# A planner that lists one core's work takes its units by shifted numbers

## The reference, cut to what matters

```python
x = x + L0(x, cond)     # shared: silu(x@w1)*(x@w3)@w2; routed: sum of gate_e * gelu(x@W1e)@W2e
x = x + L1(x, cond)     # the same with two shared experts
# L2, for t = 0..255, h0 = cond:
gate = sigmoid(h @ Wh.T + z_t @ Wz.T + b)
h = tanh(h * leak + gate * z_t)          # the output of step t
x = x + hs
# L3, 16 heads of 8 features:
scores = q @ k.T / sqrt(8); softmax over keys that are not later; out = attn @ v
x = x + out @ c_proj_w + c_proj_b
```

## Time and profile before

| | us |
|---|---|
| time, median of 3 runs (439.58 to 440.62) | 439.76 |
| the profiled execution's own time | 439.82 |
| its span, first to last instruction | 437.8 |
| PE busy | 414.9 (95%) |
| DVE busy | 291.6 (67%) |
| ACT busy | 249.4 (57%) |
| POOL busy | 86.2 (20%) |
| first and last SCAN start | 43.7 and 339.2 |

### The profile page before, as it was taken

One profiled execution on the slowest core, in us unless ns is written; L12 is line 12 of the kernel. 1 busy time (PEld: TensorE's weight loads), 2 busy tenths in 40 slices (PEclk: granted clock), 3 DMA queues, 4 the chain that ended last, 5 costly groups with the idle time before them and its releaser, 6 DMA issues.

```text
span 437.8 us, 13080 instructions
## 1 busy us (share of the span) xinstructions
PE 414.9 (95%) x4568; PEld 306.4 (70%) x4568; DVE 291.6 (67%) x983; ACT 249.4 (57%) x869; POOL 86.2 (20%) x366
## 2 busy tenths in 40 slices
PE   2999999899999999999999999899999999999994
PEld 2777877767777778777566767657765776777772
DVE  5875665877566665666458766447753987996662
ACT  3642664554663664654755447575657555756881
POOL 6320321231231331222322123121111000000000
PEclk9999999999999999999999999999999999999998
DMA  8510000000000000000000000000000100100001
GB/s 299 199 20 9 5 1 1 1 2 1 1 2 1 1 2 2 1 1 1 2 1 0 2 3 3 0 2 4 2 2 3 26 3 6 24 4 4 10 23 25
DMA packets 11222, 7.70 MB, mean 18 GB/s; under 512 B 8983, under 2 KB 10263, under 8 KB 11159
## 3 DMA queue, kind: packets, MB, share of 16 engines
q1 hardware_dynamic: 10727, 6.61, 4.9%
q10 hardware_dynamic: 432, 0.27, 0.2%
HBM read 5.39 MB, written 1.05 MB: 15 GB/s over the span
## 4 chain that ended last, share of the span: by engine, by line
PE 80%; ACT 9%; DVE 7%; issue 2%; DMA 1%; POOL 1%; DVEq 0%; ACTq 0%
PE ybk L1068 18%; PE cbk L1242 12%; PE hid L1221 10%; PE ybk L1193 6%; PE vbk L1221 4%; DVE cbk L1568 3%; PE hid L1119 3%; PE cbk L1246 2%; PE hid L1094 2%; ACT hb L916 2%; PE hid L1169 2%; ACT dd L990 2%; PE hid L1053 2%; PE cbk L1169 2%; ACT hs L995 1%
## 5 line engine op out<-in xcount | busy, mean ns | idle before, releaser
L1568 DVE TENSOR_TENSOR_SCAN cbk<-dd 128x24 f32<-128x24 f32 x256 | 55.6, 217 | 100.3 <-ACT dd L990 96.8
L1242 PEld LDWEIGHTS cbk<-hs,rec 128*128 128x128 f32 x512 | 76.3, 188 | 55.8 <-ACT hs L995 47.3
L1068 PE MATMUL ybk<-hg,down 128*128 128x256 f32 x352 | 100.3, 400 | 0.8 <-DVE hg L1447 0.5
L806 POOL TENSOR_TENSOR dd<-hs,leak 128x8 f32<-128x8 f32 x256 | 55.7, 218 | 229.2 <-ACT hs L995 225.5
L1242 PE MATMUL cbk<-hs,rec 128*128 128x8 f32 x512 | 92.5, 253 | 4.7 <-ACT hs L995 1.8
L995 ACT ACTIVATE hs<-cbk 128x8 f32<-128x8 f32 x256 | 45.3, 177 | 65.6 <-DVE cbk L1568 64.4
L990 ACT ACTIVATE dd<-cbk 128x8 f32<-128x8 f32 x256 | 46.4, 181 | 55.6 <-PE cbk L1242 54.6
L1221 PE MATMUL hid<-xsp,up 128*128 128x256 f16 x486 | 70.9, 277 | 0.4 <-DVE lg L1386 0.3
L1068 PEld LDWEIGHTS ybk<-hg,down 128*128 128x128 f32 x352 | 58.7, 191 | 6.3 <-DVE hg L1447 1.6
L1221 PEld LDWEIGHTS hid<-xsp,up 128*128 128x128 f16 x486 | 46.7, 106 | 8.7 <-issue 0.7
L1447 DVE TENSOR_TENSOR hg<-hb,hid 128x512 f32<-128x512 f32 x50 | 33.5, 676 | 2.6 <-PE hid L1053 2.5
(11 more groups left out here) (235 smaller groups left out, 658.2 us busy)
## 6 DMA issues: line engine op xcount, KB each, us to landing
qz<-up_in SPq DMA_DIRECT2D x3, 512.0 KB, 7.4
out_dram<-silu SPq DMA_DIRECT2D x4, 256.0 KB, 3.1
x<-x_in SPq DMA_DIRECT2D x7, 128.0 KB, 9.4
down<-down_in SPq DMA_DIRECT2D x1, 768.0 KB, 9.6
att<-att_in SPq DMA_DIRECT2D x1, 743.0 KB, 10.7
down<-down_in SPq DMA_DIRECT2D x1, 640.0 KB, 6.1
kp<-mrow SPq DMA_DIRECT2D x32, 4.0 KB
qz<-rows SPq DMA_DIRECT2D x32, 2.0 KB, 1.7
```

The source lines that it names most:

```text
L806: tts(dd[:, t % ZR, 1, :, 2], hs[:, t, :], leak[:, 0:1].broadcast_to([P, B]), ALU.mult).then_inc(decay, 1)
L1068: m = pe.matmul(ybk[l][:, 0:n], D(l, "w2" if shared else "e2", e * f + i), hg[:, hg_of[made] % NHG, i * n:i * n + n], start=first and i == ...
L1242: pe.matmul(cbk[c % 2][:, o:o + B], wh, hs[:, t, :], start=False, stop=True, skip_group_check=True).then_inc(gate_pre, 1)
L1568: nc.vector.tensor_tensor_scan(vps[chunk_of(t) % 2], dd[:, t % ZR, 0].rearrange("p b o -> p (b o)"), dd[:, t % ZR, 1].rearrange("p b o -> ...
```

## The change

A table LATER is added, with one signed shift for each *block* of units, 246 of them. `block_of()` says which block a unit belongs to: most kinds by chunk and layer, or by quarter and pair of batches. A unit's number becomes its place plus its block's shift, and at least 0. Nothing else is changed: the units, what each needs, the costs, the order inside a queue and the steps' number -1 stay. The four lists come out in another order, and with them the PSUM banks, the buffer turns, the counts in the waits and the fillers. Shifts go from -589 to 791. The core of the diff (the lines left out hold more shifts of the same kind):

```diff
--- before.py
+++ after.py
@@ -69,6 +69,50 @@
 ENGINES = ("pe", "act", "dve", "pool")
 SLACK = {"pe": .1, "act": .05, "dve": .05, "pool": .1}
 WINDOW = {"pe": .88, "act": .45, "dve": .88, "pool": .88}
+LATER = {('A', 0, 0): -4, ('A', 0, 1): -40, ('A', 0, 2): 10, ('A', 0, 3): 8, ('A', 1, 0): -21, ('A', 1, 1): -3,
...
+         ('AV', 0, 0): -18, ('AV', 0, 1): -405, ('AV', 0, 2): 28, ('AV', 0, 3): -151, ('AV', 1, 0): 261,
...
+         ('C', 0): -271, ('C', 2): 22, ('C', 3): -216, ('C', 4): 20, ('C', 5): -365, ('C', 7): -16,
+         ('E', 0, 0): -519, ('E', 0, 1): -580, ('E', 1, 0): 1, ('E', 1, 1): 9, ('E', 2, 0): -14, ('E', 2, 1): 24,
...
+         ('E', 6, 1): 12, ('E', 7, 0): 19, ('E', 7, 1): -177, ('G', 0, 0): -159, ('G', 0, 1): -123, ('G', 1, 0): 8,
...
+         ('IK',): 34, ('K', 0): -54, ('K', 2): 44, ('K', 3): -200, ('M', 0, 0): -391, ('M', 0, 1): -299,
+         ('M', 1, 0): 8, ('M', 1, 1): 8, ('M', 2, 0): 11, ('M', 3, 1): -23, ('M', 4, 0): 2, ('M', 5, 0): 8,
...
+         ('O', 2): 174, ('O', 3): -16, ('Q', 0): -5, ('Q', 1): -30, ('Q', 2): 33, ('Q', 3): -161, ('QZ', 0): -58,
...
+         ('W',): 63, ('X', 0, 0): -126, ('X', 0, 2): 93, ('X', 0, 3): 29, ('X', 1, 0): 4, ('X', 1, 1): -74,
+         ('X', 2, 0): 1, ('X', 2, 1): 462, ('X', 2, 2): 4, ('X', 2, 3): 791, ('X', 3, 0): -216, ('X', 3, 1): -18,
...
+         ('Y', 2, 0, 'e'): -24, ('Y', 2, 0, 's'): -17, ('Y', 2, 1, 'e'): -21, ('Y', 2, 1, 's'): -15,
+         ('Y', 3, 0, 'e'): 389, ('Y', 3, 0, 's'): -22, ('Y', 3, 1, 'e'): 384, ('Y', 3, 1, 's'): 391,
...
+         ('YL', 3): -31, ('YL', 5): 97, ('YL', 6): -81, ('YL', 7): 78, ('Z', 0): 10, ('Z', 1): 76, ('Z', 2): -17,
+         ('Z', 3): -19, ('Z', 4): 60, ('Z', 5): 149, ('Z', 6): 2, ('Z', 7): -14}


 def columns(*parts):
@@ -174,12 +218,35 @@
     return {"XS": 15.0, "IK": 25.0, "MB": 12.0}.get(key[0], 7.0)


+
+def block_of(key):
+
+    k = key[0]
+    if k in ("R", "RT", "RS", "RD", "RC", "RG", "GT"):
+        return "G", key[1], key[2]
+    if k in ("SA", "SB"):
+        return "SH", key[1], key[2]
+    if k == "Y":
+        return key[:4]
+    if k in ("E", "M", "YE", "AC", "X"):
+        return key[:3]
+    if k in ("K", "KP", "Q", "QP", "V"):
+        return k[0], key[1]
+    if k == "X3":
+        return k, key[1] // QT
+    if k in ("MT", "L", "EI"):
+        return "MT", key[1], key[2]
+    if k in ("A", "S", "SC", "AV"):
+        return "S" if k == "SC" else k, key[1], key[2] // 2
+    return key[:1] if k in ("VI", "W") else key[:2]
+
+
 def schedule(units):

     chain = [(kind, t) for t in range(T) for kind in ("DECAY", "STEP", "GATE", "SCAN", "NEW")]
     needs, banked, number, queues = {}, set(), {}, {}
     for n, (key, bank, need) in enumerate(units):
-        needs[key], number[key] = need, n
+        needs[key], number[key] = need, max(0, n + LATER.get(block_of(key), 0))
         if bank:
             banked.add(key)
     for key in chain:
```

## The result

The changed kernel takes 424.23 us (median of 4 runs, 423.10 to 426.60), beside 440.16 us (439.58 to 440.62) for the kernel before. The ratio is 0.965 with an interval of 0.960 to 0.969: 15.9 us less, where 5.2 us less was forecast. The profiled execution is the slowest of the four (426.60 us, span 424.8 us), so its rows show 13.2 us of the gain; the other three took 2.3 to 3.5 us less.

A forecast was written before the change was run, and what follows sets the result against it. Bound by the front, the steps' latency and work left after the last step; -0.5 (front) - 5.2 (work beside steps) + 1.0 (step length) - 0.5 (tail) = -5.2 us from 439.82 gave 434.6 us, range 429.0 to 442.5 us.

The forecast's parts named there:

- late chunk: Recurrence: chunk 3's delayed Y makes its chunk 3 us too late and stops the steps; 442.8 us, chance 0.10.
- nothing: Whole kernel: the same units compete and leftover lumps go to the next slot; time stays at 439.8 us, chance 0.10.
- more switches: PE: finer mixing adds ten weight-load waits between tiled and full units, 0.3 us each; 442.8 us, chance 0.08.
- Front: Before the first step: chunk 0's units win ties, steps start sooner; -0.5 us, bounds 2 us gain and 1 us loss.
- Length of the steps: The 256 recurrence steps: fuller slots add under three more overfull ones; +1.0 us, bounds -1 and +4 us.
- Work beside the steps: Slots between steps, 220 to 339.5 us: better mixing saves half the fillers' 10.5 us of PE; -5.2 us.
- the tail's sum: After the last step: tail shorter than 93.5 us from 98.6; wrong if shrinking much less or more than fillers x 0.107 us.
- signs of being right: Second-part fillers 50 or fewer, last SCAN within 1.5 us of 339.2, tail under 93.5 us, first SCAN 42.5 to 43.7 us.
- Tail: After the last step: earlier K and Q of quarter 3 let ACT's exps start sooner; -0.5 us, bounds -3 and +2 us.
- More of the same: Steps and front: four fifths of the fillers' time (8.4 us) plus 1 us from the front; 430.4 us, chance 0.14.

The follow-up runs named there:

- the searched table: New table of 226 shifts, searched on the planner's estimate with corrected costs, fillers left out, against the kernel before: 420.97 us, ratio 0.958.
- the end fillers of the searched kernel: 14 fillers added in the waits of the last X, TR and O to the newly searched order with 54 fillers: 421.44 us, ratio 0.958 to the kernel before.
- the one with 54 fillers in its emptiest slots: Newly searched order with 54 fillers, only where work between two steps is below 0.4 us, against the kernel before: 420.80 us, ratio 0.957.

## Why the prediction was wrong, step by step

**Sign and mechanism were right.** The latency of the steps plus the work left over sets the time; an order moves work from the tail beside the steps. The runs carry that through: over all profiled executions, the tail is PE's busy time in it plus 5.7 to 7.8 us (98.6 and 92.2, 101.8 and 94.0, 96.3 and 90.3, 88.2 and 81.6, 85.4 and 77.9, 81.4 and 75.2). The late chunk, nothing and more switches did not happen.

**Front, forecast -0.5 us:** -1.0 us, inside its bounds, but executions of one order differ by up to 0.7 us there. The run with the experts' shifts alone had it at 41.9, 1.8 us sooner. The prediction misread one pair of entries: the shifts of chunk 1's first Y block are -6 and -78, not -61 and -78, so only its routed part gets 0, the shared one 62.

**Length of the steps, forecast +1.0 us:** +1.2 us, a match that owes something to luck. The forecast put three more overfull slots where attention work runs, behind 220 us; there the steps took 1.184 us each (119.6 / 101) after 1.183. The growth came before it: 177.3 / 155 = 1.144 us after 1.137. And other executions of the same order gave 296.9 and 297.8 us where this one gave 296.7. The run without fillers shows that the 69 that are left cost 2.4 us of the steps' length, and the prediction had given fillers no price. The table load still stands in the steps, at 250.15 instead of 274.13.

**Work beside the steps, forecast -5.2 us, is the step that failed.** With the tail's own -0.5 us it was to shorten the tail by 5.7 us; it shortened by 13.2, more than the bound of 10.5 us. Three things were mis-sized, in this order:

1. I took half of a bound. The fillers of the second stage fell from 98 to 49, which is exactly that half, 49 x 0.107 = 5.2 us. This part came out as written.
2. The bound left out the first stage. The prediction named its 5.5 us of fillers and gave them to a rival. They fell from 51 to 20: 3.3 us more. Work of the experts that is done sooner lets attention's run sooner, so that stage counts in the end too; that link is argued, with 64 matmuls of Y behind 220 us before and 60 now as its only sign. With it the sum is 8.6 us.
3. There was room in which no filler stood, and a filler may be worth more than 0.107 us. PE's busy time in the tail fell by 92.19 - 77.88 = 14.3 us, 5.7 us more than the 8.6; against the 75.15 us that the same 1632 matmuls took at 0.98 it fell by 17.0 us. Beside the steps, PE's idle time went from 295.50 - 288.12 = 7.38 us to 296.70 - 291.76 = 4.94 us, and the steps became 1.2 us longer: 2.4 + 1.2 = 3.6 us of room that no filler stood for, which makes 12.2 us. The rest lies in the size of a filler. As busy time the 149 fillers took 8.46 + 16.15 = 24.6 us, 0.165 us each, and the 69 took 11.5 us; 13.1 us less instead of 8.6 makes 16.7 us in all. A part of a filler's busy time overlaps the next matmul's, so 12.2 and 16.7 us are the two ends of this count, and where in between a filler's true size puts it stays open. No run varied the fillers' 0.62 us by itself. The 0.73 us of the earlier trace rows lie 0.11 us above it, 28 us over 256 slots, but with 7.4 us of idle time in the whole stage most of that wasn't free.

What was to show the tail's sum wrong, that it shrinks by much more than the fillers x 0.107 us, is what happened. All signs of being right came true as well: 49 fillers, the last SCAN 0.2 us from where it was, a tail under 93.5 us, the first SCAN at 42.7 us. They had no upper end, so they could not tell a gain of 5.2 us from one of 15.9. In the profiled execution the tail shrank by 1.1 us less than PE's work in it (13.2 against 14.3 us), as PE stood idle for 7.5 us of it instead of 6.4; what the clock of 0.94 costs is already in the 77.88 us.

**Tail, forecast -0.5 us:** the reason given, K and Q of quarter 3, was worth nothing. The overlap of the engines in the tail is no better than before, as these 6.4 and 7.5 us show.

**A late chunk:** the shift has its effect, C is 4.5 us later and 6 of 10.5 us of slack are gone, but no step waited. I had counted a loss of 12 steps; the argument against the rival, that the buffers run dry and leave Y alone, would explain why it was less, but no trace was read for it. I had not seen that the same shift could be needed for the gain.

**More switches:** PEld's waits for issue in the tail, all rows of that view added, were 9.2 us in 37 and are 10.6 us in 34. The prediction's "12 for 3.7 us" added only the two rows and was too low. Three of the largest rows after:

```profile
PEld ybk L1260 <- issue: 3.9, 10, 1.3
PEld cbk L1266 <- issue: 1.1, 2, 0.9
PEld cbk L1186 <- issue: 0.7, 4, 0.2
```

There are no more such gaps than before. Part of the 3.9 us is a single gap of 1.16 us before AV at 413.28. The Trainium skill, page TensorEngine Tiling (Array Packing), section Key Properties, says that a change of tiling mode drains TensorE; the gaps of 0.2 to 0.3 us agree, and no run here shows that the new order pays for more of them. The Trainium skill, page Perfetto Trace Analysis, section Optimization Strategy, says that interleaving regimes with different most contended engines may help. The trace agrees: beside the steps, where no engine but the latency sets the pace, DVE's busy time rose from 187.1 to 201.8 us with PE's matmuls, and in the tail it fell from 74.3 to 60.3.

**The chances.** "More of the same", four fifths of all fillers, had 0.14 and was the nearest case, and still 6 us short. I had the ends of all terms at 423.3 us and ruled them out because "fuller slots and longer steps go together". They did, but by 1 us against 14.

What stays open: which picks of the walk make the difference; no run tells. That the planner's estimate keeps the ranking nearly (405.8, 416.2, 418.1, 419.4, 422.6, 423.8, 424.8 against 424.2, 432.1, 437.3, 435.8, 440.8, 440.2, 445.0 us) says that a fit on it transfers to the chip, 16 to 20 us too low; but the searched table, 407.0 by corrected costs, brought no more than leaving the fillers out. Whether 420.8 us is near the floor of this tiling is not known.

## What to carry to other kernels

Where a greedy planner sets the order, don't price its entries one by one: the tail's PE busy time and the number of matmuls beside the latency-bound part say what an order is worth, and even a random perturbation of its tie-breaks can win 2%. Bound the gain by all the unused time of the scarce engine in the whole latency-bound part, the busy time of its fillers and its idle time (24.6 + 7.4 us here), not by a slot price for the fillers of one half of it. After such a change try the fillers again: with full slots they cost more than they brought here, with emptier ones they held the clock. And look at what the kernel beside it really did before a run is called a test: the end fillers of the searched kernel held a clock that had not fallen.

## What the runs showed of the hardware that was not expected

- 69 filler matmuls of 128x256 cost the steps 2.4 us (296.7 against 294.3 us), 0.035 us each, in one execution of each; without them the granted clock stayed at 1.00 beside the steps. In the old order, leaving out the 149 cost 5.3 us, with a granted clock of 0.65 to 0.87 in seven stretches of 10 us.
- The clock at the end of the kernel differs from one order and execution to another: the last pair of O took 2.05 us in the profiles of the changed kernel (granted clock 0.50 there), of the one with one shift set to 0 and of the searched one without fillers, 1.44 us without quarter 3's shifts and 1.10 us in the others without end fillers. Fillers that held it (1.12 us) made no difference that shows: 424.99 us with them, 424.23 us without.
- The spread of a kernel's runs followed its mean clock: 419.50 us at 0.992 and 423.84 us at 0.977 for one kernel, and 420.72 to 421.69 us at 0.993 to 0.999 for the one with 54 fillers in its emptiest slots.
